# First four tiles of a local attention: inverse roots by ScalarE's logarithm and exponential with a Newton step on GpSimd, and GpSimd's clearing in a later step

## The reference

```
h = shift_token(x)                      # half of the channels from the token before
q, k, v = split(h @ wqkv)               # 8 heads of 64
q = q / max(norm(q), 1e-12) * q_scale   # the inverse root of a sum of squares, per head
k = k / max(norm(k), 1e-12) * k_scale
q, k = rotary_xpos(q, k)                # q*cos + rotate_half(q)*sin
o = local_attention(q, k, v)            # windows of 64, each sees itself and the one before
x = x + o @ wo
```

## Time and profile before

| | us |
|---|---|
| three runs | 722.24, 723.47, 726.06 |
| median | 723.47 |
| the profiled execution | 724.43 |
| its span in the trace | 722.6 |

### The profile page before, as it was taken

The page is one execution under the profiler, slowest core; times in us unless marked ns, Lnnn a source line. Parts: engine busy times, 40 slices in busy tenths (PEclk is TensorE's granted clock), DMA queues, the critical chain, the costliest instruction groups (busy, mean ns, idle before and its releaser), DMA issues.

```text
span 722.6 us, 16005 instructions
## 1 busy us (share of the span) xinstructions
PE 626.0 (87%) x5547; PEld 433.4 (60%) x5547; DVE 567.9 (79%) x1451; ACT 489.3 (68%) x1423; POOL 386.1 (53%) x425
## 2 busy tenths in 40 slices
PE   2799997888999979998999997997899999997533
PEld 1366654555666666564666666665677777776312
DVE  5667778797999976869999997655677777777586
ACT  1578775687888883559888888343677777865333
POOL 5848767898999931668999993111012121112300
PEclk9999999999999999999999999999799999999775
DMA  7700000110111110012111110000000000000002
GB/s 227 172 2 1 1 5 9 23 24 16 24 24 28 26 60 16 6 22 53 24 23 24 24 31 16 1 2 0 1 1 2 1 2 1 2 2 1 0 0 59
DMA packets 20219, 17.28 MB, mean 24 GB/s; under 512 B 7234, under 2 KB 15884, under 8 KB 20044
## 3 DMA queue, kind: packets, MB, share of 16 engines
q1 hardware_dynamic: 19308, 16.25, 9.1%
q10 hardware_dynamic: 832, 0.00, 0.1%
HBM read 8.91 MB, written 1.05 MB: 14 GB/s over the span
## 4 chain that ended last, share of the span: by engine, by line
PE 43%; POOL 32%; DVE 10%; ACT 7%; issue 7%; DMA 0%; POOLq 0%; SPq 0%; DVEq 0%; ACTq 0%
POOL rsk L500 7%; POOL rsq L500 6%; POOL rot L617 5%; POOL rot L604 5%; PE PS L994 4%; POOL rot L610 4%; PE PS L1019 3%; POOL btmp L495 3%; PE PS L882 3%; PE PS L900 3%; PE PS L901 3%; PE PS L975 3%; PE PS L1004 3%; ACT pc L1296 2%; PE PS L967 2%
## 5 line engine op out<-in xcount | busy, mean ns | idle before, releaser
L1223 ACT ACTIVATE pc<-PS,nb,rsq 128x128 f32<-128x128 f32 x256 | 113.9, 462 | 1.0 <-DVE nb L1605 0.3
L808 PE MATMUL PS<-wqkv,hB 128*128 128x512 f32 x192 | 104.2, 626 | 3.9 <-DVE rsin L1591 1.6
L1296 ACT ACTIVATE pc<-PS,nb 128x256 f32<-128x256 f32 x128 | 59.0, 473 | 46.7 <-DVE nb L1787 46.7
L500 POOL TENSOR_TENSOR rsk<-btmp,neghalf 128x8 f32<-128x8 f32 x32 | 59.9, 1873 | 5.9 <-POOL btmp L495 5.9
L817 PEld LDWEIGHTS PS<-ident,rot 128*128 128x128 f32 x256 | 31.7, 143 | 47.9 <-issue 28.5
L1787 DVE TENSOR_REDUCE nb<-PS 128x2 f32<-128x512 f32 x64 | 40.8, 679 | 24.1 <-PE PS L994 24.1
L500 POOL TENSOR_TENSOR rsq<-btmp,neghalf 128x8 f32<-128x8 f32 x32 | 54.0, 1688 | 5.9 <-POOL btmp L495 5.9
L1614 DVE TENSOR_TENSOR pc<-pc,rden 128x512 f32<-128x512 f32 x64 | 53.4, 835 | 2.2
L1223 ACT ACTIVATION_READ_ACCUMULATOR pc<-PS,nb,rsq 128x1 f32 x256 | 53.2, 208 | 0.0
L1587 DVE TENSOR_TENSOR rot<-PS,xeff 128x512 f32<-128x512 f32 x64 | 44.1, 689 | 10.2 <-ACT sq L1211 9.6
L1601 DVE TENSOR_REDUCE mx<-PS 128x4 f32<-128x512 f32 x64 | 43.6, 681 | 8.5 <-PE PS L835 8.5
(11 more groups left out here) (236 smaller groups left out, 1719.8 us busy)
## 6 DMA issues: line engine op xcount, KB each, us to landing
V<-V SPq DMA_DIRECT2D x48, 128.0 KB, 2.2
wqkv<-in_L_ffn_wqkv SPq DMA_DIRECT2D x2, 768.0 KB, 5.4
out<-x SPq DMA_DIRECT2D x4, 256.0 KB, 2.3
x<-in_x SPq DMA_DIRECT2D x1, 768.0 KB, 6.8
ctxT<-in_ctxT SPq DMA_DIRECT2D x1, 768.0 KB, 6.8
w<-in_L_ffn_w SPq DMA_DIRECT2D x2, 341.0 KB
ctxs<-in_ctx SPq DMA_DIRECT2D x1, 576.0 KB, 8.6
gel<-in_bands SPq DMA_DIRECT2D x1, 512.0 KB, 8.9
```

The costliest lines, as they stand in the source:

```text
L500: return tt(dst, tmp, neghalf[:, 0, 0:tmp.shape[1]], ALU.pow)
L808: i = mm(ps, hB[:, b % 2, j * P:(j + 1) * P], wqkv[:, w * INNER:(w + 1) * INNER], start=True, stop=True)
L1223: i = af(pc[:, g % 2, par, c * P:(c + 1) * P], c_bank(g, par)[:, c * P:(c + 1) * P], ACT.Exp, bias=nb[:, g % 2, at], scale=rsq[:, g % 8, 2 ...
L1296: i = af(pc[:, u % 2, par, n * S:(n + 1) * S], c_bank(u, par)[:, n * S:(n + 1) * S], ACT.Exp, bias=nb[:, u % 2, par * 2 + n:par * 2 + n + ...
```

## The change

Four things change.

First, `rest_of_constants()` is called in GpSimd's step u = 1, behind the third batch's norms, and no longer between `a_rstd(0)` and `a_rstd(1)`.

Second, for tiles 0 to 3 of the first layer GpSimd calls `b_turned_first` in place of `b_turned_k` and `b_turned_q`. It waits for the sums of squares of k and of q, clips both with one instruction, adds k and q, waits for ScalarE's roots, does one Newton step (four instructions over 128x16) and multiplies k. ScalarE's new `b_roots` computes exp(-0.5 ln(ss)).

Third, the order of pieces in local steps before 0 becomes t, k, q and then kT, v, qT, and in step 0 t, k and then kT, v, qT, q (`b_order`). ScalarE's `b_roots` stands there between the copies of v and of qT.

Fourth, ScalarE's first preloaded table is a set that has both functions. The rsk and rsq buffers become one, rsqk; the other tiles' roots stay as they were.

```diff
+ROOTS = B_AHEAD["k"]
+def b_order(layer, step):
+    if layer == 0 and step < 0:
+        return ["t", "k", "q"], ["kT", "v", "qT"]
+    if layer == 0 and step == 0:
+        return ["t", "k"], ["kT", "v", "qT", "q"]
+    return B_MID, B_END
...
             a_rstd(0)
-            rest_of_constants()
             a_rstd(1)
...
                 elif b + 2 < B:
                     a_norm(b + 2)
+                if u == 1:
+                    rest_of_constants()
...
+            def b_turned_first(g):
+
+                pool.wait_ge(sem("B_kss"), g + 1)
+                pool.wait_ge(sem("B_qss"), g + 1)
+                sg, r = ss[:, g % 2], rsqk[:, g % 8]
+                ts(sg, sg, 1e-24, None, ALU.max).then_inc(sem("B_clip"), 1)
+                for name in ("k", "q"):
+                    _, k, turn = b_piece(name, g)
+                    pool.wait_ge(bank_free[k], 2 * turn + 2)
+                    m = rot[:, g % 2 * 2 + int(name == "q"), :]
+                    tt(m, m, rsin[:, int(name == "q"), :], ALU.add).then_inc(sem("B_ksum" if name == "k" else "B_q"), 1)
+
+                pool.wait_ge(sem("B_root"), 2 * g + 2)
+                tt(root[:, 0], r, r, ALU.mult).then_inc(sem("B_newton"), 1)
+                pool.wait_ge(sem("B_newton"), 3 * g + 1)
+                tt(root[:, 1], root[:, 0], sg, ALU.mult).then_inc(sem("B_newton"), 1)
+                pool.wait_ge(sem("B_newton"), 3 * g + 2)
+                ts(root[:, 0], root[:, 1], -0.5, 1.5, ALU.mult, ALU.add).then_inc(sem("B_newton"), 1)
+                pool.wait_ge(sem("B_newton"), 3 * g + 3)
+                tt(r, r, root[:, 0], ALU.mult).then_inc(sem("B_qrs"), 1)
+                pool.wait_ge(sem("B_qrs"), g + 1)
+                pool.wait_ge(sem("B_ksum"), g + 1)
+                r3 = rot[:, g % 2 * 2, :].rearrange("p (h d) -> p h d", h=H)
+                tt(r3, r3, r[:, 0].unsqueeze(2).broadcast_to([P, H, DH]), ALU.mult).then_inc(sem("B_k"), 1)
...
-                if 0 <= u - A_UNITS + B_AHEAD["k"] < T:
+                if 0 <= u - A_UNITS + B_AHEAD["k"] < ROOTS:
+                    b_turned_first(u - A_UNITS + B_AHEAD["k"])
+                elif ROOTS <= u - A_UNITS + B_AHEAD["k"] < T:
                     b_turned_k(u - A_UNITS + B_AHEAD["k"])
                     b_turned_q(u - A_UNITS + B_AHEAD["k"])
...
-            nc.scalar.preload_act_table_set("exp_and_others")
+            nc.scalar.preload_act_table_set("natural_log_exp_and_others")
...
+            def b_roots(g):
+
+                r = rsqk[:, g % 8]
+                act.wait_ge(sem("B_clip"), g + 1)
+                af(r, ss[:, g % 2], ACT.Ln).then_inc(sem("B_root"), 1)
+                act.wait_ge(sem("B_root"), 2 * g + 1)
+                af(r, r, ACT.Exp, scale=-0.5).then_inc(sem("B_root"), 1)
...
-                pieces("kT", "v", "qT", "q")
+                if layer == 0 and step < 0:
+                    pieces("q", "kT", "v")
+                    if g + B_AHEAD["k"] >= 0:
+                        b_roots(g + B_AHEAD["k"])
+                    pieces("qT")
+                else:
+                    pieces("kT", "v", "qT", "q")
```

More of the change, by code:

```diff
@@ L136 @@
     number("A", a_pieces(A_MID, u) + a_pieces(A_END, u))
-    number("B", b_pieces(B_MID, 0, u - A_UNITS))
+    number("B", b_pieces(b_order(0, u - A_UNITS)[0], 0, u - A_UNITS))
     if u - A_UNITS == T - 3:
         number("F", [("u", 0)])
-    number("B", b_pieces(B_END, 0, u - A_UNITS))
+    number("B", b_pieces(b_order(0, u - A_UNITS)[1], 0, u - A_UNITS))
     number("F", f_tail(0, u - A_UNITS))
@@ L271, in program @@
         rs = sb("rs", [P, 4])
-        rsq = sb("rsq", [P, 8, H])
-        rsk = sb("rsk", [P, H])
+        rsqk = sb("rsqk", [P, 8, 2, H])
+        root = sb("root", [P, 2, 2, H])
         av = sb("av", [P, 3, 10 * D])
@@ L605, in b_turned_k @@
                 pool.wait_ge(sem("B_kss"), g + 1)
-                rsqrt(rsk[:], ss[:, g % 2, 0, :], btmp[:, 0, :], 1e-24, ALU.max, "B_ktmp", g + 1).then_inc(sem("B_krs"), 1)
+                rsqrt(rsqk[:, g % 8, 0], ss[:, g % 2, 0, :], btmp[:, 0, :], 1e-24, ALU.max, "B_ktmp", g - ROOTS + 1) \
+                    .then_inc(sem("B_krs"), 1)
                 pool.wait_ge(sem("B_ksum"), g + 1)
-                pool.wait_ge(sem("B_krs"), g + 1)
+                pool.wait_ge(sem("B_krs"), g - ROOTS + 1)
                 r3 = r.rearrange("p (h d) -> p h d", h=H)
-                tt(r3, r3, rsk[:].unsqueeze(2).broadcast_to([P, H, DH]), ALU.mult).then_inc(sem("B_k"), 1)
+                tt(r3, r3, rsqk[:, g % 8, 0].unsqueeze(2).broadcast_to([P, H, DH]), ALU.mult).then_inc(sem("B_k"), 1)
             def b_turned_q(g):
@@ L907, in b_step @@
                     b_turn(layer * T + step)
-                for name, g in b_pieces(B_MID, layer, step):
+                for name, g in b_pieces(b_order(layer, step)[0], layer, step):
                     b_make(name, layer, g % T)
@@ L917, in b_step @@
                     f_up(layer * 4, 1)
-                for name, g in b_pieces(B_END, layer, step):
+                for name, g in b_pieces(b_order(layer, step)[1], layer, step):
                     b_make(name, layer, g % T)
@@ L1223, in b_exps @@
                     i = af(pc[:, g % 2, par, c * P:(c + 1) * P], c_bank(g, par)[:, c * P:(c + 1) * P], ACT.Exp,
-                           bias=nb[:, g % 2, at], scale=rsq[:, g % 8, 2 * c + par:2 * c + par + 1], accum_out=den[:, g % 2, at])
+                           bias=nb[:, g % 2, at], scale=rsqk[:, g % 8, 1, 2 * c + par:2 * c + par + 1], accum_out=den[:, g % 2, at])
                 i.then_inc(e_full[par], 1)
@@ L1604, in b_max @@
                 dve.wait_ge(sem("B_qrs"), g + 1)
-                tt(nb[:, g % 2, at], mx[:, g % 2, at], rsq[:, g % 8, par::2], ALU.mult).then_inc(nb_full[par], 1)
+                tt(nb[:, g % 2, at], mx[:, g % 2, at], rsqk[:, g % 8, 1, par::2], ALU.mult).then_inc(nb_full[par], 1)
             def b_scale(g, par):
```

2 lines of the change are left out of this document (1 added, 1 removed).

## The result

| | before | after |
|---|---|---|
| median, 20 runs each | 723.95 us | 728.12 us |
| lowest and highest | 721.54, 727.53 | 725.47, 730.49 |
| span of the profiled execution | 722.6 us | 726.5 us |
| granted clock of TensorE, mean | 0.958 | 0.954 |

The change makes the kernel slower: by 4.2 us between the medians, and by a ratio of 1.0049 (95% interval 1.0035 to 1.0063; 3.5 us), which is formed over all the runs and not from the two medians. Two things of opposite sign are in the trace: a gain of 2.4 us at the start and a loss of 6.4 us in the first tiles of local attention; the spans differ by 3.9 us.

A forecast was written before the change was run, and what follows sets the result against it. GpSimd was taken to bound local attention from tile 7 on, at 8.57 us a tile, so its start time mattered. Terms -2.4 + 0.1 + 3.7 + 1.0 = +2.4 us gave 725.9 us, range 719.0 to 731.0.

The forecast's parts named there:

- likeliest case: Whole kernel: the forecast's own sum of terms, +2.4 us on the profiled execution, giving a median of 725.9 us.
- (c): Start and later step: the load eats the early gain (-1.4) and the moved clearing costs +1.0; 727.8 us, chance 0.10.
- (b): Tiles 0 to 3: ScalarE's wait starves TensorE, its clock falls twice in the loop; +5.4, 728.9 us, chance 0.25.
- The clearing, -2.4 and +0.1: Moved clearing: -2.4 us at the start as VectorE's normalisations are unblocked, +0.1 us at its new place.
- The wait for the context: Start: VectorE would wait from 12.85 to 13.9 us for the context's second part, probably covered; 1.05 us if not.
- Prices of small instructions: Roots, per tile: GpSimd's clip and four small instructions 1.7 us (1.2 to 3.4), ScalarE's two functions 0.65 us (0.45 to 1.0).
- The serial loop: Tiles 0 to 3: clip, logarithm and copies follow one another, TensorE waits; tile 7 starts 3.7 us later (+2 to +6).
- walk: Local attention: step-by-step timing at full clock from tile 0's q sums to later tiles, ending +3.7 us at tile 7.
- the clock's term: Local attention's first tiles: TensorE's granted clock falls behind its new idle time; half of one fall, +1.0 us (0 to +4).
- the wait that was to shrink: GpSimd at tile 6: its wait for q would shrink from 1.51 to 0.35 us, giving back part of the delay.
- (a): First four tiles: GpSimd's saving comes through, 5 us given to it; 716 us, chance 0.13.
- (d): Tiles 0 to 3: GpSimd's small instructions cost 3.4 us, each tile 1.7 us longer, +3 to +7; 730 us, chance 0.05.

The follow-up runs named there:

- experiment 1: The kernel before with only GpSimd's six clearings moved to step u = 1: 721.13 us against 724.15 us for the kernel before, ratio 0.9958.
- experiment 4: The changed kernel plus 24 unread TensorE products where TensorE waits for tile 0's copies: 724.89 us against 724.15 us for the kernel before, ratio 1.0006.

## Why the prediction was right, and where it was off

The predicted time was 725.9 us in a range of 719.0 to 731.0; measured were 728.1 us. The side was right (0.3% slower forecast, 0.5% measured) and the range held it. The result lies not on the likeliest case but beside my rivals (c), 727.8 us, and (b), 728.9 us.

**The clearing, -2.4 and +0.1.** Right in mechanism and size: the first transposition 2.46 us sooner, experiment 1 faster by 3.0 us (1.4 us either way). That tile 0's sums came 2.37 us sooner, right to the tenth, is luck in part, since these sums scatter by 1.6 us between kernels with the same code. The wait for the context came (0.72 us) and was covered, as argued from the sums of squares behind it. At the new place the trace shows 0 and not +0.1: the product wasn't blocked.

**Prices of small instructions.** Clip to the next start 112.28 - 112.06 = 0.22 us, the four of the Newton step 116.03 - 114.73 = 1.30 us: 1.5 us where I took 1.7. The nearest row, a clip of 128x12, was a good neighbour. ScalarE's roots, 112.72 - 112.35 = 0.37 us, lay below my lower bound of 0.45: the exponential starts 0.25 us behind the logarithm, and the copy 0.12 us behind the exponential's start. The count of table loads stayed, 6 in either trace. With all terms a little below their value the sum could not have come out above it by them.

**The serial loop.** Copies predicted at 115.25 - 2.4 = 112.85 us, found at 112.72; TensorE's idle time predicted 4.3 us, found 4.22. The walk from q's sums to the next tile's, from tile 0 on, was made at full clock, and these are the ends:

| sums of tile | walk | changed kernel | experiment 4, no fall at tile 0 |
|---|---|---|---|
| 1 | 10.7 us | 13.0 us | 10.4 us |
| 2 | 21.6 us | 24.1 us | 21.6 us |
| 3 | 33.8 us | 35.9 us | 34.0 us |
| 4 | 46.5 us | 48.2 us | 47.9 us |

Against experiment 4 the walk is right within 0.3 us up to tile 3. Against the changed kernel it misses 2.3 us in the first tile, and 2.5, 2.1 and 1.7 us in all by the next three: the whole miss arose in the first. GpSimd's waits ahead of the clips were 3.75, 6.21 and 3.57 us where I had given 2 and twice 4 to 6: the first is longer by the slow TensorE, the last is shorter than I gave, which cost nothing.

**The step that failed: the clock's term.** I took +1.0 us, "half of one fall", because a fall of 4 us can cost up to 2 us. (The falls of before lasted 3.4 us each, not 4.) Here the first fall lasted 6.8 us, and every product in it stood on the loop. From the values' start to the end of k and q TensorE took 121.40 - 113.89 = 7.5 us, and 120.07 - 115.40 = 4.7 us in experiment 4: 2.8 us in TensorE's work, of which 2.3 to 2.5 us reached the next sums. The clock fell again near 148 us, within the loop, and near 172 us. I had named that as what would make my forecast wrong ("if the granted clock is low more than once between tile 0 and tile 7"), though loosely: the kernel before has two such falls there too. What counts is the fall right ahead of work on the path. I had the mechanism and its place, and gave it a quarter of the chances; the idle 4.3 us that I had worked out myself, right ahead of work that lies on the path, spoke for the whole price.

**A second term was off: the wait that was to shrink.** How much later each k add comes, counted from tile 0's q sums:

| k add of | before | walk | changed kernel | lost, walk | lost, measured |
|---|---|---|---|---|---|
| tile 4 | 36.0 us | 40.1 us | 42.3 us | 4.2 us | 6.4 us |
| tile 5 | 47.7 us | 52.2 us | 54.1 us | 4.5 us | 6.4 us |
| tile 7 | 65.4 us | 69.1 us | 71.8 us | 3.7 us | 6.4 us |

The loss is whole by tile 4, 1.9 us over the walk at tile 5, and this is where the clock's term belongs. (Experiment 4, without the fall at tile 0 but with its own two later ones, has tile 5's k add at 53.8 us, also 1.6 us over the walk: how the 1.9 us divide between the falls is open.) Behind tile 5 my walk gave 0.8 us back, because GpSimd's wait at tile 6 would shrink from 1.51 to 0.35 us. (By these figures it should have been 1.16: 4.5 - 1.16 is 3.3 and not 3.7, a slip of 0.4 us in my sum.) The wait did shrink, to 0.75 us, but two other instructions of GpSimd there took longer, tile 5's q add 1.72 in place of 1.28 us and tile 6's first power 1.96 in place of 1.67 us, and nothing came of it. So the 2.7 us that the distance has over the walk are 1.9 us where I had 1.0 for the clock, and 0.8 us that were not given back. With them the sum is -2.4 + 3.7 + 2.7 = +4.0 us, beside 3.9 us between the spans. Why those two instructions were longer is open.

**Rivals.** (a) asked for the saving of GpSimd to come through; its idle time ahead of each clip shows that it didn't, and ScalarE's copies could not come before the sums, as the rows had said. (c) is nearest in number, and that is luck: both of its terms fell. (d) fell: the small instructions were cheap. (b) is what came in kind, a fall at tile 0 and one at the roots of tile 3. Its price, 2 us for each, was not measured as such: the first cost 2.3 to 2.5 us, the second has no experiment.

## What to carry to other kernels

Giving a loaded engine's work to one with time to spare pays only if the helper does not stand waiting, in its own fixed order, ahead of something that a third engine needs: price the wait at the helper first, by the row of what stands behind it, and the work second. Where a new wait leaves TensorE idle for some us right ahead of work that is on the path, price that work at the lower clock (here 7.5 in place of 4.7 us) and not at half of it; and look for a part of a change that pays alone, as here the clearing's move does (721.1 us).

## What the runs showed of the hardware that I had not expected

- 24 products that nobody reads, 2.78 us of TensorE in a wait of 4.2 us, kept the granted clock at 1.00 and made the kernel 3.1 us faster than the changed one. The other falls moved: they came near 136 and 153 us, and no longer near 148 and 172 us.
- A logarithm and an exponential of 128x16 that depends on it hold ScalarE for 0.37 us together, less than two of their own durations (0.22 and 0.21 us).
- A product of two SBUF inputs (128x1) ran in 0.16 us beside GpSimd's clearing of 1.80 us, where two tensor-scalar instructions over 128x128 had been held up for 2.45 us beside a row of clearings; with the clearings gone from there they take 0.60 us (experiment 1).
